# Layer norm scales of tiles 0 to 6 made in the stage before, with Newton's steps on VectorE in place of ScalarE's root

## What is computed

```python
def _layernorm(x, axis=-1, eps=1e-05):
    m = jnp.mean(x, axis=axis, keepdims=True)
    v = jnp.var(x, axis=axis, keepdims=True)
    return (x - m) / jnp.sqrt(v + eps)

x = x + _L0_xattn_ref(_layernorm(x), ctx_512, ctx_512, ...)   # cross attention, 16 heads
x = x + _L0_attn_ref(_layernorm(x), ...)                      # state space block (mamba2 form)
x = x + _L0_ffn_ref(_layernorm(x), ...)                       # FFN, 4 of 16 blocks per token by a router
x = x + _L1_xattn_ref(_layernorm(x), ctx_512, ctx_512, ...)   # cross attention, one head
x = x + _L1_attn_ref(_layernorm(x), ...)                      # causal self attention
x = x + _L1_ffn_ref(_layernorm(x), ...)                       # gated FFN with quantized values
```

## Time and profile before

| what | value |
|---|---|
| median of 3 runs | 1695.85 us (1692.62 to 1696.95) |
| the profiled execution | 1692.85 us |
| its span (first to last instruction) | 1691.1 us |
| mean granted clock of TensorE, 1 = full | 0.969 |
| busy share: PE, DVE, ACT, POOL | 92%, 70%, 53%, 43% |
| `cross0` | 0 to 850.7 |
| `state_space` | 850.7 to 990.3 |
| `block_ffn` | 990.3 to 1210.8 |
| `cross1` (its block of queries ends at 1238.9) | 1210.8 to 1385.8 |
| `self1` | 1385.8 to 1442.3 |
| `quant_ffn` | 1442.3 to 1691.1 |

### The profile page before, as it was taken

One profiled execution on the slowest core, in us unless ns is written; L12 is line 12 of the kernel. 1 busy time (PEld: TensorE's weight loads), 2 busy tenths in 40 slices (PEclk: granted clock), 3 DMA queues, 4 the chain that ended last, 5 costly groups with the idle time before them and its releaser, 6 DMA issues. The chain is left out here.

```text
span 1691.1 us, 33888 instructions
## 1 busy us (share of the span) xinstructions
PE 1557.8 (92%) x13881; PEld 815.0 (48%) x13990; DVE 1180.3 (70%) x1952; ACT 888.4 (53%) x1189; POOL 723.6 (43%) x348
## 2 busy tenths in 40 slices
PE   6999999999999999999888989999889989799469
PEld 3445555555555555555444564344534444444124
DVE  6588888888888888887557458998622233526981
ACT  1487777777777777777463224431212222326650
POOL 1478888888787888886306813320000000000000
PEclk9999999999999999999999979999899999999779
DMA  4489999999999999999925653569779934000001
GB/s 140 128 182 192 190 192 194 186 198 188 194 193 198 195 182 198 191 190 171 185 70 156 225 226 79 143 175 209 233 311 398 393 143 188 1 1 0 1 0 50
DMA packets 555526, 282.73 MB, mean 167 GB/s; under 512 B 481760, under 2 KB 533472, under 8 KB 552304
## 3 DMA queue, kind: packets, MB, share of 16 engines
q1 hardware_dynamic: 555376, 280.63, 70.0%
HBM read 138.74 MB, written 22.54 MB: 95 GB/s over the span
## 5 line engine op out<-in xcount | busy, mean ns | idle before, releaser
L572 POOL TENSOR_TENSOR x<-x_prob,x 128x1604 bf16<-128x1604 f32 x120 | 388.1, 3234 | 143.3 <-ACT x L737 143.3
L867 DVE TENSOR_REDUCE x_negmax<-x_score 128x1 f32<-128x1604 f32 x128 | 233.6, 1825 | 17.3 <-PE x_score L613 7.2
L727 ACT ACTIVATE x_prob<-x_score,x_negmax 128x1604 f32<-128x1604 f32 x128 | 204.8, 1600 | 25.4 <-DVE x_negmax L867 20.7
L596 PE MATMUL x_ring<-x_ctx_hi,wk_split 128*128 128x400 bf16 (+1 forms) x1024 | 216.2, 333 | 0.3 <-DVE x_kT L795 0.3
L596 PE MATMUL x_ring<-wv_split,x_ctx_hi 128*128 128x512 bf16 (+1 forms) x770 | 200.3, 379 | 9.7 <-issue 7.3
L795 DVE SCALAR_TENSOR_TENSOR x_kT<-x_ring,bk,x_kT 128x400 bf16<-128x400 f32 (+1 forms) x256 | 162.2, 634 | 31.8 <-ACT x_kT L716 23.8
L737 ACT CAST x<-x_prob 128x1604 bf16<-128x1604 f32 x120 | 183.0, 1525 | 0.0
L801 DVE TENSOR_TENSOR x_v<-x_ring,x_v 128x512 bf16<-128x512 f32 (+1 forms) x208 | 143.7, 691 | 52.8 <-ACT x_v L720 50.0
L716 ACT ACTIVATE x_kT<-x_ring,bk 128x400 bf16<-128x400 f32 (+1 forms) x196 | 116.4, 594 | 91.2 <-PE x_ring L596 90.3
L720 ACT CAST x_v<-x_ring 128x512 bf16<-128x512 f32 (+1 forms) x148 | 86.5, 585 | 96.9 <-PE x_ring L596 96.9
L596 PEld LDWEIGHTS x_ring<-x_ctx_hi,wk_split 128*128 128x128 bf16 x1024 | 93.8, 97 | 87.0 <-issue 19.8
(11 more groups left out here) (347 smaller groups left out, 2399.9 us busy)
## 6 DMA issues: line engine op xcount, KB each, us to landing
y_ctx<-in_ctx SPq DMA_DIRECT2D x16, 1664.0 KB, 10.5
y_ctxT<-in_ctxT SPq DMA_DIRECT2D x16, 1601.0 KB, 13.7
x_stage<-in_ctxT SPq DMA_DIRECT2D x48, 400.0 KB, 4.4
x_q_rows<-q_rows SPq DMA_DIRECT2D x64, 128.0 KB, 3.1
m_xT<-in_L_ffn_w SPq DMA_DIRECT2D x16, 512.0 KB, 4.5
ffn_w_parts<-m_xT SPq DMA_DIRECT2D x32, 256.0 KB, 2.7
x_stage<-in_ctxT SPq DMA_DIRECT2D x16, 401.0 KB, 4.9
f_w<-ffn_w_parts SPq DMA_DIRECT2D x4, 1024.0 KB, 8.6
```

Source lines behind the costliest of these rows:

```text
L572: pool.tensor_tensor(ph[:, g % 2, 1, 0:NKP], prob[:, g % 2, :], ph[:, g % 2, 0, 0:NKP], ALU.subtract).then_inc(pl_done, 1)
L596: last = pe.matmul(out_, lhs, rhs, start=(i == 0), stop=(i == len(steps) - 1))
L727: nc.scalar.activation(prob[:, g % 2, :].rearrange("p (c n) -> p c n", n=QW), scores, ACT.Exp, bias=nmax[:, g % 2:g % 2 + 1], accum_out=rs ...
L867: dve.tensor_reduce(nmax[:, pair % 2:pair % 2 + 1], scores, mybir.AxisListType.XY, ALU.max, negate=True).then_inc(max_done, 1)
```

## The change

`Kit.norm_scales(dve, first, last, step, base)` is new. On VectorE it makes mean, variance, scale and shift of tiles `first` to `last`: one bn_aggr for each tile, then 13 small instructions, each of which waits for the one before: the epsilon; a first guess of the reciprocal root by integer arithmetic on the float's bits (a shift, then a multiply-add); three Newton steps of three instructions each; the shift. It is called twice for each of the five later norms:

- for tiles 0 to 6, in the stage that ends, on VectorE directly ahead of the addition of tile 7 (in `cross0` ahead of the wait for TensorE's product of that tile, in `cross1` at the head of the last round). It waits for the bn_stats of tile 6, for which `tile_stats` now counts a semaphore.
- for tile 7, in the next stage, behind the normalization of tiles 0 to 3 (`last_scales_on_vector`, 14 instructions on 128 x 1), with a wait for its last one. What stands behind it on VectorE: the normalization of tiles 4 to 7 in `state_space` and `block_ffn`, the copies of turned tiles in `cross1` and `self1`, the largest absolute value in `quant_ffn`. ScalarE waits for it ahead of tile 7 only.

ScalarE's square root is gone from these five norms, and with it eight loads of an activation table: five stood ahead of the root (L180, L2282), and three ahead of the exponential of `block_ffn` (L1470), `cross1` (L1839) and `self1` (L2002), whose table now stays loaded. The loads of `state_space` (L1163, L1182) and of `quant_ffn`'s sigmoid (L2313) stay. Means, scales and shifts now lie in tensors that live through the kernel.

The diff, cut to its core (the call in `state_space` stands for those in `block_ffn` and `self1`):

```diff
+ROOT_SEED = 1597463007.0
+I32 = mybir.dt.int32
...
-    def tile_stats(self, dve, x, t, done):
+    def tile_stats(self, dve, x, t, done, counted):
         dve.wait_ge(*done)
         if isinstance(t, int):
-            dve.bn_stats(self.stats[:, t, :], x[:, t, :])
+            dve.bn_stats(self.stats[:, t, :], x[:, t, :]).then_inc(counted, 1)
...
+    def norm_scales(self, dve, first, last, step, base):
+
+        ve, r, u = self.meanvar[:, first:last, 1], self.rstd[:, first:last, 0], self.shift[:, first:last]
+        if base:
+            dve.wait_ge(step, base)
+        for t in range(first, last):
+            dve.bn_aggr(self.meanvar[:, t, :], self.stats[:, t, :]).then_inc(step, 1)
+        done = base + last - first
+        dve.wait_ge(step, done)
+        dve.tensor_scalar(ve, ve, EPS, None, ALU.add).then_inc(step, 1)
+        dve.wait_ge(step, done + 1)
+        dve.tensor_scalar(r.bitcast(I32), ve.bitcast(I32), 1, None, ALU.logical_shift_right).then_inc(step, 1)
+        dve.wait_ge(step, done + 2)
+        dve.tensor_scalar(r.bitcast(I32), r.bitcast(I32), -1.0, ROOT_SEED, ALU.mult, ALU.add).then_inc(step, 1)
+        done += 3
+        for _ in range(3):
+            dve.wait_ge(step, done)
+            dve.scalar_tensor_tensor(u, r, -0.5, r, ALU.mult, ALU.mult).then_inc(step, 1)
+            dve.wait_ge(step, done + 1)
+            dve.tensor_tensor(u, u, ve, ALU.mult).then_inc(step, 1)
+            dve.wait_ge(step, done + 2)
+            dve.scalar_tensor_tensor(r, u, 1.5, r, ALU.add, ALU.mult).then_inc(step, 1)
+            done += 3
+        dve.wait_ge(step, done)
+        dve.scalar_tensor_tensor(u, self.meanvar[:, first:last, 0], -1.0, r, ALU.mult, ALU.mult).then_inc(step, 1)
...
+    LAST_SCALES = 14
+
     def on_vector(self, dve):
-        self.small_on_vector(dve)
-        self.hat_on_vector(dve, range(NT))
+        if self.loaded:
+            self.small_on_vector(dve)
+            self.hat_on_vector(dve, range(NT))
+        else:
+            self.hat_on_vector(dve, range(NT // 2))
+            self.last_scales_on_vector(dve)
+            self.hat_on_vector(dve, range(NT // 2, NT))
+
+    def last_scales_on_vector(self, dve):
+        self.k.norm_scales(dve, NT - 1, NT, self.s_var, 0)
+        dve.wait_ge(self.s_var, self.LAST_SCALES)
...
     def on_scalar(self, nc, act):
-        self.root_on_scalar(nc, act)
-        act.wait_ge(self.s_shift, 1)
         for t in range(self.HALF, NT):
+            if t == NT - 1:
+                act.wait_ge(self.s_var, self.LAST_SCALES)
             nc.scalar.activation(self.xhat[:, t, :], self.x[:, t, :], ACT.Identity, bias=self.shift[:, t:t + 1],
...
     def on_vector(self, dve):
-        self.small_on_vector(dve)
-        dve.scalar_tensor_tensor(self.shift[:], self.meanvar[:, :, 0], -1.0, self.rstd[:, :, 0], ALU.mult,
-                                 ALU.mult).then_inc(self.s_shift, 1)
         self.hat_on_vector(dve, range(self.HALF))
+        self.last_scales_on_vector(dve)
         for t in self.BY_VECTOR:
...
                             elif t == 0:
                                 dve.wait_ge(ring_free, BIAS + 1)
+                            elif t == NT - 1:
+                                k.norm_scales(dve, 0, NT - 1, stats_done, NT - 1)
                             dve.wait_ge(ring_full, g + 1)
...
             for t in range(NT):
+                if t == NT - 1:
+                    k.norm_scales(dve, 0, NT - 1, s_stats, NT - 1)
                 dve.wait_ge(s_xo, NT)
                 dve.wait_ge(s_o, t + 1)
                 dve.tensor_tensor(x[:, t, :], x[:, t, :], banks[6 + t % 2][:], ALU.add).then_inc(s_out, 1)
-                k.tile_stats(dve, x, t, (s_out, t + 1))
+                k.tile_stats(dve, x, t, (s_out, t + 1), s_stats)
...
+                if not scores:
+                    k.norm_scales(dve, 0, NT - 1, s_stats, NT - 1)
                 if products:
...
-            norm.small_on_vector(dve)
-            dve.scalar_tensor_tensor(shift[:], norm.meanvar[:, :, 0], -1.0, norm.rstd[:, :, 0], ALU.mult,
-                                     ALU.mult).then_inc(s_shift, 1)
             norm.hat_on_vector(dve, range(NT // 2))
+            norm.last_scales_on_vector(dve)
             dve.wait_ge(norm.s_hat, NT // 2)
```

More of the change, by code:

```diff
@@ L124, in __init__ @@
         self.s_xT = k.sem(ctx, name + "_xT_done")
+    LAST_SCALES = 14
     def on_vector(self, dve):
-        self.small_on_vector(dve)
-        self.hat_on_vector(dve, range(NT))
-    def small_on_vector(self, dve):
-        before = NT if self.loaded else 0
-        if self.loaded:
-            for t in range(NT):
-                dve.wait_ge(*self.loaded(t))
-                dve.bn_stats(self.stats[:, t, :], self.x[:, t, :]).then_inc(self.s_stats, 1)
-            dve.wait_ge(self.s_stats, before)
+        if self.loaded:
[8 more added lines that the diff above has]
+        dve.wait_ge(self.s_var, self.LAST_SCALES)
+    def small_on_vector(self, dve):
+        before = NT
+        for t in range(NT):
+            dve.wait_ge(*self.loaded(t))
+            dve.bn_stats(self.stats[:, t, :], self.x[:, t, :]).then_inc(self.s_stats, 1)
+        dve.wait_ge(self.s_stats, before)
         for t in range(NT):
@@ L178, in root_on_scalar @@
     def root_on_scalar(self, nc, act):
+        if not self.loaded:
+            return
         act.wait_ge(self.s_var, 1)
@@ L2280, in _ @@
         def _(act):
-            act.wait_ge(norm.s_var, 1)
-            nc.scalar.activation(norm.small[:, 1, :], norm.small[:, 0, :], ACT.Sqrt).then_inc(norm.s_root, 1)
-            act.wait_ge(s_shift, 1)
             for t in range(NT // 2, NT):
-                nc.scalar.activation(xhat[:, t, :], x[:, t, :], ACT.Identity, bias=shift[:, t:t + 1],
+                if t == NT - 1:
+                    act.wait_ge(norm.s_var, norm.LAST_SCALES)
+                nc.scalar.activation(xhat[:, t, :], x[:, t, :], ACT.Identity, bias=k.shift[:, t:t + 1],
                                      scale=norm.rstd[:, t, :]).then_inc(s_hat2, 1)
```

37 lines of the change are left out of this document (22 added, 15 removed).

## The result

| | before | after |
|---|---|---|
| median of 11 runs each, taken together | 1693.90 us | 1699.99 us |
| lowest to highest | 1692.62 to 1696.95 | 1697.52 to 1704.25 |
| profiled execution, its time | 1692.85 us | 1703.96 us |
| its span, its granted clock | 1691.1 us, 0.969 | 1702.2 us, 0.962 |

The ratio is 1.0045, with the interval 1.0033 to 1.0057: 7.6 us slower (5.6 to 9.7), over the bound of 0.3%. The time came out as forecast (1700.2); the difference did not, which was to be +4.3 us. The two fit only because the three runs of before on which the forecast stood have a median of 1695.85, 2 us above that of all eleven.

A forecast was written before the change was run, and what follows sets the result against it. Between stages VectorE's scales were taken as the bound, with TensorE busy 92% of the span. Barrier terms +2.5, +1.1, -2.4, 0 and +3.1 gave +4.3 us on a median of 1695.85: 1700.2 us, range 1695.0 to 1704.5.

The forecast's parts named there:

- The steps at 0.20 and 0.19 us: Small VectorE instructions: each step costs 0.20 us in the first group (3.1 us), 0.19 in the second (2.7 us).
- Barrier 1, +2.5: `cross0` to `state_space`: the group delays the barrier 2.5 us; load `wG` moves along, so the head start gives nothing.
- Barrier 2, +1.1: `state_space` to `block_ffn`: the group outlasts the idle time, so the barrier and the five loads come 1.1 us later.
- Barrier 3, -2.4: `block_ffn` to `cross1`: idle time hides the group, no load stands in the way, products start 2.4 us earlier.
- Barrier 4, 0: `cross1` to `self1`: idle time hides the group, but products wait for load `wv` anyway; no gain or loss.
- Barrier 5, +3.1: `self1` to `quant_ffn`: no idle time, so the barrier comes 3.2 us later and little is regained; +3.1 us.
- The table loads, 0: ScalarE: eight table loads of 1.28 us leave, counted as no gain in kernel time.
- the clock: Rival: longer TensorE pauses in `state_space` and `block_ffn` prolong 1.2 GHz, +1.4 us beyond the sum, +5.7 in all; chance 0.20.
- theory A: Whole kernel: the time changes by the sum of the barrier terms alone, +4.3 us for the change.

The follow-up runs named there:

- changed_again: The changed kernel run and profiled once more with no edit (the second execution): 1699.20 us against 1693.26 before, ratio 1.0051.
- only_state_space: Only the scales of `state_space` made early, the other four norms as before (a single part of the change): 1697.00 us against 1693.49 before, ratio 1.0023.
- six_steps: The change with six Newton steps instead of three in both groups: 1711.16 us against 1693.26 before, ratio 1.0108.
- newton_in_stage: Against before: all eight tiles' scales made behind the barrier by Newton's steps on VectorE, nothing early: 1696.09 us against 1693.26, ratio 1.0017.
- only_quant_ffn: Only the scales of `quant_ffn` made early, the other four norms as before: 1696.82 us against 1693.49 before, ratio 1.0025.
- early_where_hidden: Early scales only for `cross1` and `self1`, the other three norms as before: 1692.77 against 1693.26 us (1.0001); again, 1691.72 against 1693.67 (0.9984).
- filled_state_space: The change with keep-busy matmuls only at the end of `cross0` and behind two turned tiles of `state_space`: 1700.10 us against 1693.67 before, ratio 1.0031.
- early_halves: Tiles 0 to 3 early for `state_space` and `block_ffn`; `cross1`, `self1` as in the change, `quant_ffn` as before: 1693.64 us against 1693.67 before, ratio 0.9997.
- split_only: Before, with first products of `state_space` and `block_ffn` waiting only for their own weights, no scales early: 1691.69 us against 1693.67, ratio 0.9984.
- filled_pauses: The change with keep-busy matmuls in five TensorE pauses, in or at the end of `cross0`, `state_space`, `block_ffn` and `self1`: 1697.75 us against 1693.49 before, ratio 1.0028.
- split_loads: Scales early as in `early_halves`, and first products waiting only for their own weights as in `split_only`: 1683.31 us against 1693.49 before, ratio 0.9947.

## Why the prediction was right and where it was not

- *The steps at 0.20 and 0.19 us.* Right. The traces have them, the integer ones too, and six steps cost what twice the chain should.
- *Barrier 1, +2.5.* Right as a place and a mechanism: `wG` still releases L1107, and the profiles of the second execution and of the single part have +2.41 and +2.17 there. The 4.00 of after has 1.5 us from ahead of the change. The pause ahead of the products grew to 2.6 and 2.9 us, not to 3.4.
- *Barrier 2, +1.1.* The group does push the addition (996.29, after the group's last step at 996.21), and the loads of `block_ffn` move with it. The stage, though, grew by 2.2 and 3.7 us in two profiles. That loads "move with the barrier" holds only roughly: `sel` ends TensorE's wait 5.4 to 6.6 us behind the barrier over the profiles that wait for it, in before 5.4, in after 6.0.
- *Barrier 3, -2.4.* Right: `cross1` is 1.3 to 2.6 us shorter in the eight profiles with its scales early by three steps, and 0.2 longer in `six_steps`, where the copies wait for the longer second group. What holds the end of `block_ffn` seems to be SP's stores, which the prediction did not name. The copies start 4.55 us behind the barrier, before 4.46.
- *Barrier 4, 0.* Right: `wv` still ends the wait.
- *Barrier 5, +3.1.* Right: +3.4 and +3.2 in `self1`, and the second group gave back only what was written.
- *The table loads, 0.* Right by `newton_in_stage`. The Trainium skill, "ScalarE: Activation LUTs", section "What ACT_TABLE_LOAD costs", has 2.66 us for a load with its drain, by which the eight would be some 21 us of ScalarE's time (an estimate). The trace of before has 1.28 us for a load, and the exponential starts at 1408.88, 0.02 us behind its end; ScalarE's busy time fell by 11.6 us in all. No gap of the second kind is seen.

**The step that fell short** is the last one of the sum, that nothing but the barriers' terms counts: the forecast gave the clock 0.20 and its own sum 0.55, and took "within 0.3%" for the likeliest. Measured is +7.6 and +8.6 us for a sum of 4.3 (by the medians 6.1 and 5.9).

What the runs show of the difference is that it goes with TensorE's mean granted clock, which every single run has on record, not only the profiled one. The last column is the measured difference (by the ratio) less the sum that theory A gave for that kernel, with 2.4 us for `cross1`:

| kernel | mean granted clock of its runs | beyond its sum, us |
|---|---|---|
| before (21, 29, 30 runs) | 0.9695, 0.9696, 0.9693 | |
| the change, again | 0.9655, 0.9664 | +3.3, +4.3 |
| `six_steps` | 0.9655 | +4.3 |
| `only_state_space`, `only_quant_ffn` | 0.9677, 0.9685 | +1.4, +1.1 |
| `early_where_hidden`, again | 0.9689, 0.9700 | +2.6, -0.3 |
| `filled_state_space`, `early_halves` | 0.9690, 0.9690 | +1.0, +1.9 |
| `newton_in_stage` | 0.9698 | +1.1 |
| `split_only`, `filled_pauses` | 0.9715, 0.9719 | -0.3, +0.4 |
| `split_loads` | 0.9737 | -1.0 |

Within the runs of the change it is the same: the five over 1702 us have a mean clock of 0.964, the six under 1700 one of 0.967. The size is possible: 0.004 less over 1700 us is 13.6 us more at 1.2 GHz, which can cost at most half of that, 6.8 us (an estimate, if TensorE had work throughout). And filling the pauses raised the clock and took the time to the bare sum. So the rival named the mechanism that the runs speak for, and its size (+5.7, or 1.0034, is within the first interval and just outside the second). It did not name the place. At the starts of the stages, where it looked, the clock rose only 1.0 and 1.5 us later behind the barrier of `state_space` in the two profiles of the change, and 0.8 later and 0.8 earlier in `block_ffn`; but both profiles have 10 us more of low clock in the middle of `state_space`. That stretch stands in three profiles of six in which all of `state_space`'s scales are early (after, `changed_again`, `filled_state_space`), and in none of the eight others. It is suggestive and no more: there is one profile of each kernel, and filling the first pause did not remove it.

That the clock is the cause, and the whole of the excess, is not shown. A longer wait of TensorE lowers the clock also where it costs nothing, the intervals of the single parts and of the filled kernel are as wide as the excess, and why the clock falls in the middle of `state_space` stays open.

## What to carry to other kernels

Work moved over a barrier gains only if idle time hides it before the barrier and nothing else holds the work behind it; read both from the trace for each place, since here one place of five met both. Where two waits end together, an edit of either is worth little and the edit of both is worth the gap (0.5 and 2.7 against 9.0 us; in `block_ffn` the first products move by nothing with one edit and by 2.9 us with both): look for a semaphore that collects loads which the first instruction does not need. And take the time before from more than three runs when the effect looked for is that of their spread, and the length of an untouched stage from more than one profile.

## What the runs showed of the hardware

- A small VectorE operation that waits for the one ahead costs 0.20 us on 128 x 7 and 0.19 on 128 x 1, whether float or integer.
- TensorE's clock can fall in the middle of a stage whose start, pauses and work are nearly unchanged, in one execution and not in another: at 918 us in `filled_state_space` it went to half behind a wait of 1.28 us, and in `filled_pauses` it stayed full behind one of 1.33. The Trainium skill, "TensorE: Matmul & The Clock Gate", section "Why this matters for your kernels", asks for short pauses between bursts. At the start of `state_space` the traces agree with it only in part: the clock rose 11.1 and 11.6 us behind the barrier in the two profiles of the change, with waits of 2.9 and 2.6 us, and 10.1 us in before, with 0.93; but 10.0, 9.5 and 9.0 us in `only_state_space`, `six_steps` and `early_halves`, with waits of 2.9, 2.8 and 3.9. In the middle of the stage the length of a wait did not tell whether the clock fell.
- In `block_ffn` of `changed_again` TensorE was at the lower level for 27.3 us between 994 and 1022 us, 23.9 in before, most of it while float32 matmuls of 128 x 128 and 128 x 16 follow one another without a pause.
- One kernel's runs spread over several us, whatever the change: 1697.5 to 1704.3 us in eleven runs of after, 1692.6 to 1697.0 in eleven of before, but 1689.2 to 1698.6 in thirty others of before. The slower runs of a kernel tend to have the lower granted clock (in the eleven of after 0.964 over 1702 us, 0.967 under 1700).
